# Cross attention's key and value projections by seven quarter products in place of eight, on one core of Trainium2

## The reference

```python
q = h @ wq + bq                      # h: layer norm of x, 64 queries a batch
k = ctx @ wk + bk                    # ctx: 512 x 512 for each of 8 batches
v = ctx @ wv + bv
att = softmax(q k^T / sqrt(32) + mask)      # layer 0 has a mask, layer 3 none
x = x + concat_heads(att @ v) @ wo + bo
```

## Time and profile before

| | |
|---|---|
| Median of 3 runs | 3578.55 us (3578.19 to 3585.3) |
| The profiled execution's span | 3577.8 us |
| Its own time | not recorded apart; the median stands 0.75 us above its span |
| TensorE busy | 3140.3 us, 88% |
| VectorE busy | 1190.4 us, 33% |
| ScalarE busy | 695.5 us, 19% |
| GpSimd busy | 137.7 us, 4% |
| Mean granted TensorE clock | 0.933 |
| Chain that ended last | DMA 13% of the span (the last stage's weights), TensorE 3% |

### The profile page before, as it was taken

How to read it: one execution, slowest core, us unless ns; L and a number is a source line. 1 busy time by engine, 2 the same in 40 slices (tenths; PEclk the granted TensorE clock), 3 DMA queues, 4 the chain that set the end, 5 groups by cost and what they waited for, 6 DMA issues and landing times. The chain is left out here.

```text
span 3577.8 us, 41207 instructions
## 1 busy us (share of the span) xinstructions
PE 3140.3 (88%) x16833; PEld 1532.5 (43%) x16833; DVE 1190.4 (33%) x2513; ACT 695.5 (19%) x1295; POOL 137.7 (4%) x182
## 2 busy tenths in 40 slices
PE   8998879997899899999899989989998997666666
PEld 4444644343444444344467665434445652111111
DVE  3555430002344569765341132113444411000000
ACT  2443101101233331111012120003342211000000
POOL 1000010001000000001000000000000100000000
PEclk9998879999999999989999999999998998888878
DMA  3101069998211022221530111981001258999999
GB/s 144 44 29 39 13 244 417 413 423 345 88 71 47 27 71 65 101 83 36 222 155 12 67 73 55 418 338 48 25 22 46 111 211 337 420 420 420 420 420 372
DMA packets 102911, 654.11 MB, mean 183 GB/s; under 512 B 19048, under 2 KB 28264, under 8 KB 39784
## 3 DMA queue, kind: packets, MB, share of 16 engines
q1 hardware_dynamic: 98064, 638.19, 44.2%
q0 software_dynamic: 4160, 13.63, 1.0%
q10 hardware_dynamic: 536, 0.14, 0.0%
HBM read 642.41 MB, written 9.50 MB: 182 GB/s over the span
## 5 line engine op out<-in xcount | busy, mean ns | idle before, releaser
L2926 PE MATMUL banks<-ring,h 128*32 128x512 f32 x1024 | 162.7, 746 | 78.8 <-DMA ring<-in_L_ffn_w 53.5
L2909 PE MATMUL banks<-ring,mine 128*32 128x512 f32 x1024 | 161.0, 692 | 60.9 <-DMA ring<-in_L_ffn_w 60.4
L1690 PE MATMUL banks<-ring,xT 128*64 128x512 f32 x736 | 166.0, 605 | 15.0 <-DMA ring<-in_L_ffn_Wu 7.1
L504 PE MATMUL banks<-normed_features,first 128*128 128x256 f32 x768 | 168.0, 379 | 1.1 <-ACT normed_features L471 1.1
L504 PEld LDWEIGHTS banks<-normed_features,first 128*128 128x128 f32 x768 | 144.6, 190 | 23.0 <-issue 3.2
L3037 DVE COPY mine<-mT 128x32 f32<-128x32 f32 x31 | 5.6, 182 | 443.0 <-PE banks L2909 443.0
L807 PE MATMUL banks<-ctxT,wkb 128*128 128x512 f32 x256 | 115.4, 596 | 2.1 <-PEq L142 2.1
L811 PE MATMUL banks<-big 128*128 128x512 f32 x256 | 116.8, 602 | 0.0
L807 PE MATMUL banks<-ring 128*128 128x512 f32 x256 | 115.5, 596 | 1.4 <-PEq L142 1.4
L811 PE MATMUL banks<-ring 128*128 128x512 f32 x256 | 115.6, 596 | 0.0
L811 PE MATMUL banks<-wvb,ctxT 128*128 128x512 f32 x256 | 115.6, 596 | 0.0
(11 more groups left out here) (613 smaller groups left out, 4851.6 us busy)
## 6 DMA issues: line engine op xcount, KB each, us to landing
ring<-in_L_ffn_w SPq DMA_DIRECT2D x256, 1024.0 KB, 27.1
ring<-in_L_ffn_Wd SPq DMA_DIRECT2D x24, 2048.0 KB, 21.0
ring<-in_L_ffn_Wg SPq DMA_DIRECT2D x23, 2048.0 KB, 23.9
ring<-in_L_ffn_Wu SPq DMA_DIRECT2D x23, 2048.0 KB, 20.9
wb<-in_L_ffn_W SPq DMA_DIRECT2D x32, 1024.0 KB, 24.1
first<-in_L_ffn_W SPq DMA_DIRECT2D x16, 1024.0 KB, 19.9
second<-in_L_ffn_W SPq DMA_DIRECT2D x16, 1024.0 KB, 22.0
ctxT<-in_ctxT SPq DMA_DIRECT2D x8, 1024.0 KB, 4.9
```

Source lines behind the costliest of these rows:

```text
L504: ins = pe.matmul(m.ps[:, self.banks[q % R], 0:256], w[:, k, mm * P:(mm + 1) * P], m.yT[:, k, 256 * half:256 * half + 256], start=(k == 0) ...
L1690: ins = pe.matmul(ps[H * side:H * side + H, 2 * kind + half, :], xT[:, p % 2, k, H * own:H * own + H], rows_of(where[(name, slot)], C)[:, ...
L2909: ins = pe.matmul(ps[B4 * q:B4 * q + B4, 0, :], mine[:, e % 2, k, :], w[:, q * 512:(q + 1) * 512], start=(k == 0), stop=(k == C - 1))
L2926: ins = pe.matmul(ps[B4 * q:B4 * q + B4, 2, :], h[:, Q * n + q, :], w[:, q * D:(q + 1) * D], start=(n == 0), stop=(n == Q - 1))
```

## The change

K and V of batches 1 to 7 are made by Strassen's scheme, one level deep. The context and each weight matrix are cut into 2 x 2 quarters of 256 x 256 (MIX = 256), and each of the two products is made of seven quarter products in place of eight. A quarter product is four fp32 products of 128x128 by 128x256, so eight passes of 256 columns, into one bank. Batch 0 keeps its eight units.

- GpSimd makes the sums and differences of quarters. Before the loop, `mix_weights` makes five quarter sums of each weight matrix (`wsum`); `mix_context` makes five of each batch's context, three into `csum` and two in place in `ctxT`.
- TensorE runs `quarter_product(b, par, n)` for n = 0 to 6 (K) and 7 to 13 (V), two in steps 0 to 2 and 4 to 6, one in steps 3 and 7, into banks 0 and 1 in turn.
- ScalarE copies products 0, 1 and 2 of each kind to `part` (with the key bias for K, in two halves, since a half has its own bias column).
- VectorE joins products 3 to 6: bank plus `part` into the target quarter of `kT` or `v`. The joins of 3 and 4 use the copies of products 1 and 2; those of 5 and 6 use offsets that GpSimd makes in `offsets`: the copy of product 0 less those of 1 and 2, plus the target quarter that the join of 3 or 4 wrote.
- The value bias is no longer added to v but, since each row of probabilities sums to 1, to the attention's output: `oT` is written by an addition of `vcol`, a column for each chunk. Its load is four column loads of 128 x 4 bytes, where it was one broadcast of 256 KB.
- The load of the context two batches ahead waits for this batch's first quarter product; SP waits for batch 0's last unit before its loop; TensorE waits for batch 0's last V copy before its loop.
- In layer 3 the stage's tensors take 13 slots of the ring where they took 9. Layer 1's call (`knorm`) keeps the old units.

```diff
+def mix_weights(pool, step, w, sums):
+    w11, w12, w21, w22 = (quarter(w, i, j) for i in range(2) for j in range(2))
+    for i, (a, b, op) in enumerate(((w11, w22, ALU.add), (w12, w22, ALU.subtract), (w21, w11, ALU.subtract),
+                                    (w11, w12, ALU.add), (w21, w22, ALU.add))):
+        ins = pool.tensor_tensor(sums[:, i], a, b, op)
+    step(ins)
...
 SP:
-                    sp.wait_ge(*projected.at(UN * b + UN))
+                    sp.wait_ge(*(multiplied.at(PROD * b + 1) if split else projected.at(UN * b + UN)))
                     sp.dma_start(ctxT[:, par], m.d["ctxT"][b + 2]).then_inc(*ctx_landed[par].up(16))
...
+            if split:
+                sp.wait_ge(*projected.at(UN))
             run(sp, body)
 GpSimd:
+            def mix_context(b, par, step):
+                pool.wait_ge(*ctx_at(par, b))
+                c11, c12, c21, c22 = (quarter(ctxT[:, par], j, i) for i in range(2) for j in range(2))
+                pool.tensor_tensor(csum[:, par, 1], c21, c22, ALU.add)
+                pool.tensor_tensor(csum[:, par, 2], c11, c12, ALU.add)
+                step(pool.tensor_tensor(csum[:, par, 0], c11, c22, ALU.add))
+                pool.tensor_tensor(c21, c21, c11, ALU.subtract)
+                pool.tensor_tensor(c12, c12, c22, ALU.subtract).then_inc(*mixed.up())
+            def offsets(b, par, kind, step):
+                n, done = 6 * b + 3 * kind, 4 + 8 * b + 4 * kind
+                pool.wait_ge(*copied.at(n + 2))
+                step(pool.tensor_tensor(part[:, 2], part[:, 2], part[:, 0], ALU.subtract))
+                pool.wait_ge(*copied.at(n + 3))
+                step(pool.tensor_tensor(part[:, 2], part[:, 2], part[:, 1], ALU.subtract))
+                for i in range(2):
+                    pool.wait_ge(*joined.at(done + i + 1))
+                    pool.tensor_tensor(part[:, i], target(kind, par, 1 - i, i), part[:, 2], ALU.add).then_inc(*offset.up())
+            def body(b, par, last, step):
+                offsets(b, 1 - par, 0, step)
+                if not last:
+                    mix_context(b + 2, par, step)
+                offsets(b, 1 - par, 1, step)
 TensorE:
+            def quarter_product(b, par, n):
+                kind, i = divmod(n, 7)
+                if n == 0:
+                    pe.wait_ge(*mixed.at(b + 1))
+                if 2 <= i < 5:
+                    pe.wait_ge(*copied.at(6 * b + 3 * kind + i - 1))
+                else:
+                    pe.wait_ge(*joined.at(8 * b + 4 * kind + (i + 3 if i < 2 else i)))
+                for r in range(2):
+                    for k in range(2):
+                        a, x = (left[:, k, r * P:(r + 1) * P], right[:, k, :]) if kind else \
+                            (right[:, k, r * P:(r + 1) * P], left[:, k, :])
+                        ins = pe.matmul(halves(n % 2)[:, r, :], a, x, start=(k == 0), stop=(k == 1))
+                ins.then_inc(*multiplied.up())
...
+            if split:
+                pe.wait_ge(*v_taken.at(KC))
...
+                    if not end and split:
+                        for n in quarters_of(j):
+                            quarter_product(b, par, n)
 ScalarE, after the exponential of a step:
+            def copy_quarters(b, par, n):
+                kind, i = divmod(n, 7)
+                if i > 2:
+                    return
+                act.wait_ge(*multiplied.at(PROD * b + n + 2))
+                if i == 0:
+                    act.wait_ge(*joined.at(8 * b + 4 * kind + 4))
+                src, dst = halves(n % 2), part[:, (2, 0, 1)[i]]
+                if kind:
+                    act.activation(dst, src, ACT.Copy).then_inc(*copied.up())
+                else:
+                    for r in range(2):
+                        bias = bsum[:, r:r + 1] if i == 0 else kbias[:, 2 * i - 2 + r:2 * i - 1 + r]
+                        ins = act.activation(dst[:, r, :], src[:, r, :], ACT.Identity, bias=bias)
+                    ins.then_inc(*copied.up())
 VectorE, after the row maximum of a step:
+            def join_quarters(b, par, n):
+                kind, i = divmod(n, 7)
+                if i < 3:
+                    return
+                dve.wait_ge(*multiplied.at(PROD * b + n + 2))
+                which = (i - 3) % 2
+                if i < 5:
+                    dve.wait_ge(*copied.at(6 * b + 3 * kind + 2 + which))
                 else:
-                    dve.tensor_tensor(v[:, par, r, :], ps[:, r % 2, :], vbias, ALU.add).then_inc(*v_taken.up())
+                    dve.wait_ge(*offset.at(4 * b + 2 * kind + 1 + which))
+                keys, cols = ((1, 0), (0, 1), (0, 0), (1, 1))[i - 3]
+                dve.tensor_tensor(target(kind, 1 - par, keys, cols), halves(n % 2), part[:, which], ALU.add)\
+                   .then_inc(*joined.up())
...
+                    ins = dve.tensor_tensor(dst, src, vcol.unsqueeze(2).to_broadcast([P, C, S]), ALU.add)
 Loads of layers 0 and 3:
-             (bv[:], d["L0_xattn_bv"].partition_broadcast(P)), (bo[:], d["L0_xattn_bo"].partition_broadcast(P))),
+             *[(b[:, 2, c:c + 1], d["L0_xattn_bv"][c * P:c * P + P].unsqueeze(1)) for c in range(C)], (bo[:], d["L0_xattn_bo"].partition_broadcast(P))),
```

More of the change, by code:

```diff
@@ L716, in cross_attention @@
     TBN = len(set(TB))
-    few = 1 if not (mask is not None or knorm) else C
+    few = 0 if not (mask is not None or knorm) else 2 if not knorm else C
+    split = not knorm
+    PROD = 14
+    wmixed, mixed, multiplied, copied = s("weights_mixed"), s("ctx_mixed"), s("quarters_product"), s("quarters_copied")
+    offset, joined, pstep = s("quarters_offset"), s("quarters_joined"), s("mix_step")
     norm, outs, head_loads, on_pool_last = head or (None, None, None, None)
@@ L722, in cross_attention, with ctx_at, target, quarters_of @@
     with m.local(inside=inside, kT=[P, 2, C, SK], v=[P, 2, KC, D], qs=[P, 2, C, S],
[L723 to L729 removed]
+                 pr=[P, R, SK], prT=[P, RP, KC, P], sc=[P, 2, SK if pre else 1], col=[P, 2, J, 4],
+                 extra=[P, max(few, 1), SK if few else 1], extraT=[P, C if knorm else 1, SK if knorm else 1],
+                 wsum=[P, 2, 5, 2, MIX if split else 1], csum=[P, 2, 3, 2, MIX if split else 1],
+                 part=[P, 3, 2, MIX if split else 1], bsum=[P, 2]) as \
+            (kT, v, qs, pr, prT, sc, col, extra, extraT, wsum, csum, part, bsum), \
+            m.block((o_taken, 1), (turned_taken, TBN), *([(multiplied, 1), (joined, 4)] if split else [])) as block:
+        ps = m.ps
+        def ctx_at(par, b):
+            return ctx_landed[par].at(8 * b + 8 * par + (0 if par else here))
+        def target(kind, par, keys, cols):
+            return quarter(v[:, par], keys, cols) if kind else quarter(kT[:, par], cols, keys)
+        def quarters_of(j):
+            first = 7 * (j // 4) + 2 * (j % 4)
+            return range(first, first + (2 if j % 4 < 3 else 1))
+        def halves(bank):
+            return ps[:, bank, :].rearrange("p (r n) -> p r n", r=2)
+        def run(eng, body, per=0, steps=vstep):
             with repeat(eng, B // 2 - 1) as i:
[L732 removed]
+                step = Chain(eng, steps, i, per) if per else None
                 body(2 * i, 0, False, step)
@@ L736, in run @@
                     step.end()
-            step = Chain(eng, vstep) if per else None
+            step = Chain(eng, steps) if per else None
             body(B - 2, 0, True, step)
@@ L829, in await_scores @@
                     pe.wait_ge(*q_spread.at(b + 1))
-                    pe.wait_ge(*k_taken.at(C * b + C))
+                    if split and not first:
+                        pe.wait_ge(*joined.at(8 * b))
+                    else:
+                        pe.wait_ge(*k_taken.at(C * b + C))
             def scores(par, g):
@@ L896, in body @@
                         scores(1 - par, 0)
[L897 removed]
+                    if not end and split:
+                        for n in quarters_of(j):
+                            quarter_product(b, par, n)
+                    elif not end:
                         for u in range(U * j, U * j + U):
@@ L970, in body @@
                         power(b + 1, 1 - par, j + 2 - J)
-                    if not end:
+                    if not end and split:
+                        for n in quarters_of(j):
+                            copy_quarters(b, par, n)
+                    elif not end:
                         for u in range(U * j, U * j + U):
@@ L1066, in body @@
                         norm_context(b + 2, step)
-                    if not end:
+                    if not end and split:
+                        for n in quarters_of(j):
+                            join_quarters(b, par, n)
+                    elif not end:
                         for u in range(U * j, U * j + U):
```

59 lines of the change are left out of this document (39 added, 20 removed).

## The result

| | median (lowest to highest) | runs |
|---|---|---|
| before | 3579.32 us (3578.19 to 3585.3) | 4 |
| after | 3541.4 us (3539.68 to 3544.13) | 4 |
| after / before | 0.9891, interval 0.9879 to 0.9904 | |

The change takes 37.9 us off, where 35.0 were forecast; the time lies 2.1 us under the predicted 3543.5. The profiled span is 3537.3 us, 40.5 less than the 3577.8 of before. A second timing of the same kernel, in the experiments, gave 3534.9 us, so the gain stands between 38 and 46 us.

A forecast was written before the change was run, and what follows sets the result against it. TensorE was taken to bound both attention loops. Gains of 22.4 us in layer 3 and 16.8 in layer 0, less 4.2 outside, made 35.0 off: 3543.5 us; forecast 3539 to 3550 (chance 0.5), wider range 3534 to 3564.

The forecast's parts named there:

- TensorE bounds both loops, fewer passes are less time: Loops of layers 0 and 3: 27.5 us a batch go, 24.3 come; 22.4 us gained per stage without waits.
- Layer 0 keeps 16.8 us: Layer 0's seven batches: gain of 3.2 us a batch less 0.8 of stalls, so 2.4 a batch, 16.8 in all.
- Stalls of 0.6 us at product 2 and 0.2 at product 9, none in layer 3: Layer 0, each batch: TensorE waits for ScalarE's copies of products 0 and 7, which stand behind exponentials; layer 3 has slack.
- GpSimd at 1.35 us an operation, never late: Both loops: 13 GpSimd operations a batch take 17.6 of 32.6 us, and all offsets and context mixes are hidden.
- 4.2 us outside the loops: Per stage, 1.0 us waiting for batch 0's last value copy and 1.1 for four column loads; together 4.2 us.
- the bytes' worth comes off: Column loads before each loop: the low bound, 0.2 us a stage in place of 1.1, with 256 KB less to load.
- VectorE's four more joins, K's copies on ScalarE, the SP queue: Both loops: joins add 2.8 us a batch on VectorE, idle over 10; no cost beyond stalls already counted.
- VectorE held by GpSimd: Rival: VectorE's 128x1 multiply and reciprocal each wait 0.7 us beside GpSimd additions; 20 us, 3563 us. Chance 0.2.
- The longer hand-over chain: Rival: products 2 and 9 wait 1 us a batch in layer 3, 1 us more in layer 0; 3557 us. Chance 0.15.
- GpSimd the bound: Rival: GpSimd above 1.94 us an operation makes V's offset late; at 2.5 us, +35, so 3614 us. Chance 0.05.
- No stall anywhere: Rival: no TensorE stall in either loop, 44.8 less 4.2 us and some 1 less at the start; 3537 us. Chance 0.1.

The follow-up runs named there:

- copy_first: The kernel after with ScalarE's copy of product 0 of K moved ahead of step 0's exponential; 3535.21 us, ratio 0.9869 to before.
- half_products: The kernel after with every quarter product cut to its first 128 features of the contraction; 3459.38 us, ratio 0.9652 to before.
- layer3_only: The kernel after with quarter products in layer 3 alone, layer 0 on old units with the value bias at the output; 3562.19 us, ratio 0.9943 to before.
- reciprocal_first: The kernel before with VectorE's reciprocal ahead of its take of the V unit in steps 4 to 7; 3583.58 us, ratio 1.0005 to before.

## Why the prediction came out right

- **TensorE bounds both loops, fewer passes are less time.** Right. The pass was costed at 216.8 ns from L504 and took 216; layer 3's period was put at 32.6 and is 32.61. This term, 22.4 us in layer 3, measured 22.9.
- **Layer 0 keeps 16.8 us.** It kept 21.1, and this is the term that was mis-sized. The new period was forecast as 33.4 and is 33.38; the step that failed is the one ahead of it, that both layers start from layer 3's 35.9. Layer 0 came from 36.4 (254.80 / 7), because step 6 waited there for the exponential of step 7, about 0.5 us in six of the seven batches. The prediction read 34.49 busy of 35 in the earlier trace rows as full. But the 0.51 us that is missing there is as long as the wait, and two starts a loop apart would have shown it.
- **Stalls of 0.6 us at product 2 and 0.2 at product 9, none in layer 3.** 0.77 us a batch was measured (33.38 - 32.61). The first was placed right: 0.7 in step 1, named after the copy of product 0. The second is 0.14 and was half right. Product 9 does lose 0.1 us (1.84 for 1.73), as ScalarE's copy of product 7 ends only at 115.89 and the product starts at 115.94; but no wait entry names it, and the length of step 5 is set by the wait at step 6's transposes for the exponential, which the prediction didn't have. `copy_first` leaves step 5 at 4.03.
- **GpSimd at 1.35 us an operation, never late.** 1.27, and the offset has 2.5 us to spare (below); three more operations cost nothing. The threshold was right in kind: eight more turn the change into a loss, at 74 us and not the 49 (12 x 4.1) of the prediction's way.
- **4.2 us outside the loops.** Half of it was right: 1.09 and 1.08 us for the V copy of batch 0. The column loads, 2.2 us in the sum, cost nothing measurable. The bound "the bytes' worth comes off" was the true case.
- **VectorE's four more joins, K's copies on ScalarE, the SP queue.** At nothing, and seen at nothing: in layer 3's 228.25 us TensorE waits for no engine. Its only entries are two of `issue`, 0.4 us together, where an iteration of the hardware loop ends.

Against the forecast 35.0 stand 44.0 in the loops less 2.2 for the waits, so 41.8, of which the unchanged stages gave and took a few us from run to run (37.9 and 46.4 in the two timings). The misses of 4.3 in layer 0 and 2.2 in the loads both went the same way, so the sum fell 6.8 us short. That the first median lies only 2.1 us from the forecast is therefore luck: the unchanged stages took back 3.9 of them in it, and the second timing, 3534.9, lies 8.6 under the forecast and under the 3539 to 3550 that had 0.5.

**The rivals.** *VectorE held by GpSimd* is refuted by the rows that it was to be read from (shortest, median and longest in ns; first and last start):

```profile
L1145 DVE TENSOR_SCALAR col<-col x64: 152/153/157, 55.1 to 317.3; 128x1 f32<-128x1 f32 x64
...
L1150 DVE RECIPROCAL col<-col x64: 152/163/166, 56.1 to 318.3; 128x1 f32<-128x1 f32 x64
```

Not one of these 128 small operations is longer than 166 ns, and several lie inside an addition of GpSimd: the multiply at 114.40 within the one that starts here,

```profile
113.90 1.26 POOL L827 TENSOR_TENSOR ctxT<-ctxT 128x512 f32<-128x512 f32 x1
...
121.18 1.28 POOL L838 TENSOR_TENSOR part<-v,part 128x512 f32<-128x512 f32 x1 [0.16 <-POOL part L835]
...
114.40 0.15 DVE L1145 TENSOR_SCALAR col<-col 128x1 f32<-128x1 f32 x1
...
124.98 0.69 DVE L1168 TENSOR_TENSOR v<-banks,part 128x512 f32<-128x512 f32 x1 [1.03 <-PE banks L913]
```

(the offset that could come late ends at 122.46, its join starts at 124.98 and waits for TensorE). The Trainium skill (SBUF — State Buffer, "Who interferes with whom") gives the exclusive lock to VectorE operations in a two-port mode or with two SBUF inputs. By its rule this kernel had nothing to fear if an operation of one element per partition doesn't use such a mode, and the trace agrees with that reading; the additions that read one input from PSUM took 0.69 us beside GpSimd, as the page has it for one SBUF input.

*The longer hand-over chain* is refuted in layer 3, where no step is longer than its products; in layer 0 it is at most the 0.14 us of step 5. *GpSimd the bound* is refuted for this amount of work and shown at eight more. *No stall anywhere* fell by 0.77 us a batch, and copy_first is nearly that case.

**One reading to be made with care.** ScalarE's rows of the stalled step of the kernel after:

```profile
97.98 0.72 ACT L1059 ACTIVATE pr<-sc,col 128x512 f32<-128x512 f32 x1 [1.46 <-DVE col L1145]
...
98.70 0.82 ACT L1046 ACTIVATE part<-banks,bsum 128x256 f32<-128x256 f32 x2
```

Step 0's transposes start 3.9 us before 98.51, and product 0 is through 2.2 us behind them, at about 96.8; ScalarE stood idle for the 1.46 us ahead of the exponential. The copy, 0.84 long, would have fitted in, and came behind only by its order in the list. An idle entry on an engine with work ready behind the waiting instruction is worth a try.

**What stays open.** Which of VectorE's and ScalarE's shares of the chain sets half_products' 30.0 us, and how much of it is the lower clock, was not separated. Unchanged stages differ by several us from kernel to kernel, and their length goes with the granted clock. By the traces' clock records TensorE was at the lower level for 235.5 us between the loops in before (2134.4 us long), 249.2 in after (2139.9), and 256.0 in `layer3_only` (2144.8), the most and the longest of all. That the clock makes the length was not tested, nor what makes it fall more often in one kernel than in another.

## What to carry to other kernels

When a loop is bound by one engine, cost the removed work in passes from a row of the same shape, and take the old period of each loop from its own first and last start: two loops of the same code with and without a mask differed by 0.5 us a batch, where all the stalls that were worked out with care came to 0.8. A scheme that trades products for sums on an idle engine has a cliff: find the due time of the last sum and count how many operations fit before it. Where an in-order engine idles ahead of an instruction that waits, look whether the next one is ready.

## What was not expected of the hardware

- TensorE went on 0.46 us after the end of the exponential that released it, at three different places of that end (195.94 to 196.40, 194.87 to 195.33, and in reciprocal_first 195.79 to 196.25), and 0.35 after it in the kernel after. In between TensorE's list passes the waits ahead of the transposes, one after another. So a chain that ends 0.3 us before TensorE is free can still be on its path, and the trace names the gap `issue` or not at all.
- GpSimd's additions of 128x512 took 1.26 to 1.28 us throughout, beside VectorE's work on PSUM and its small operations; the earlier trace rows had medians of 1.45 and 1.72 for the same form.
- A load that was issued 1.4 us later landed 0.7 earlier, since 256 KB ahead of it were gone: 5.0 us from issue to landing instead of 7.1.
- With half the products layer 0's loop was granted 0.91 of the clock, with waits of TensorE of up to 2.4 us in it; layer 3's loop, with waits of 1.3 us at most, kept 1.00. With eight more additions on GpSimd both loops were at 0.94, with one wait of 4.4 to 4.6 us a batch.
